# One attention and expert kernel on one core: products of the previous batch, kv and transposes put at other units, and stacking transfers in two pieces

## What is computed

```python
xn = layernorm(x)                                   # x: 8 x 512 x 256
q, k, v = split(xn @ W_qkv.T)                       # 16 heads of 16
q_p = elu(einsum('bhnd,hdf->bhnf', q, proj)) + 1    # 128 features per head
k_p = elu(einsum('bhnd,hdf->bhnf', k, proj)) + 1
kv = einsum('bhnf,bhnd->bhfd', k_p, v)
attn = einsum('bhnf,bhfd->bhnd', q_p, kv)
attn = attn / (einsum('bhnf,bhf->bhn', q_p, k_p.sum(2)) + 1e-8)
a = attn @ W_out.T + b_out
# each token goes to the two best of 8 experts (softmax over the two), 256 -> 1024 -> 256, exact gelu
x + a + ffn(xn)
```

## Time and profile before

| | |
|---|---|
| median of three runs | 743.44 us (743.26 to 744.01) |
| the profiled execution, its own time | 743.44 us |
| its span, first to last instruction | 741.3 us |
| mean granted TensorE clock | 0.993 |
| PE, PEld, DVE, ACT, POOL busy | 95%, 83%, 66%, 64%, 30% of the span |
| transfers | 91.64 MB, mean 124 GB/s |

### The profile page before, as it was taken

How to read it: one execution, slowest core, us unless ns; L and a number is a source line. 1 busy time by engine, 2 the same in 40 slices (tenths; PEclk the granted TensorE clock), 3 DMA queues, 4 the chain that set the end, 5 groups by cost and what they waited for, 6 DMA issues and landing times.

```text
span 741.3 us, 17723 instructions
## 1 busy us (share of the span) xinstructions
PE 704.8 (95%) x5617; PEld 618.0 (83%) x5618; DVE 492.8 (66%) x1281; ACT 476.1 (64%) x879; POOL 223.9 (30%) x165
## 2 busy tenths in 40 slices
PE   8799999999999998799999999999999999999995
PEld 4667777767676866389999999999899999999995
DVE  8898989898989878655556664445666444466443
ACT  5587878787878786675476744456674444666451
POOL 2314141505050504602342222233223323322222
PEclk9999999999999999899999999999999999999998
DMA  8856473737474647526355352334535223443321
GB/s 258 213 140 169 105 222 100 225 98 227 95 229 93 205 96 238 216 89 186 74 82 173 54 157 48 58 76 61 179 55 160 52 44 73 74 132 68 54 44 22
DMA packets 44037, 91.64 MB, mean 124 GB/s; under 512 B 6897, under 2 KB 30193, under 8 KB 41729
## 3 DMA queue, kind: packets, MB, share of 16 engines
q1 hardware_dynamic: 28258, 59.36, 28.3%
q0 software_dynamic: 13872, 18.75, 14.5%
q10 hardware_dynamic: 1872, 13.11, 4.9%
HBM read 39.32 MB, written 26.67 MB: 89 GB/s over the span
## 4 chain that ended last, share of the span: by engine, by line
PE 62%; DVE 19%; issue 10%; ACT 6%; ACTq 1%; DVEq 1%; POOLq 0%
PE F L481 9%; PE F L483 9%; PE F L482 9%; DVE qp L1398 4%; DVE kp L1398 3%; PE NUM L481 3%; PE NUM L482 3%; PE NUM L483 3%; ACT h L1151 3%; PE DEN L481 3%; PE DEN L482 3%; PE DEN L483 3%; PE DEN L555 2%; PE F L543 2%; PE F L537 2%
## 5 line engine op out<-in xcount | busy, mean ns | idle before, releaser
L1151 ACT ACTIVATE h<-F,b1c 128x384 f32<-128x384 f32 x200 | 110.8, 574 | 163.8 <-PE F L483 148.3
L1820 POOL DMA_INDIRECT out<-ysb,icur x75 | 120.4, 1605 | 302.9 <-DVE ysb L1664 288.1
L1641 DVE TENSOR_TENSOR hl<-h,hh 128x768 fp32r<-128x768 f32 x100 | 95.9, 959 | 156.4 <-ACT hh L1155 156.4
L996 ACT ACTIVATE e_ring<-F 128x512 f32<-128x512 f32 x256 | 146.3, 624 | 41.4 <-PE F L537 31.8
L481 PE MATMUL F<-gxh,wh 128*128 128x384 f32 (+1 forms) x400 | 129.8, 325 | 3.9 <-ACT h L1151 1.7
L483 PE MATMUL F<-gxh,wl 128*128 128x384 f32 (+1 forms) x400 | 128.3, 321 | 0.0
L482 PE MATMUL F<-gxl,wh 128*128 128x384 f32 (+1 forms) x400 | 128.3, 321 | 0.0
L1761 POOL DMA_INDIRECT xg<-rows,slots x64 | 63.6, 994 | 179.4 <-PE F L537 144.8
L1398 DVE SCALAR_TENSOR_TENSOR kp<-F,e_ring 128x512 f32<-128x512 f32 x128 | 82.7, 681 | 18.3 <-PE DEN L555 10.5
L1398 DVE SCALAR_TENSOR_TENSOR qp<-F,e_ring 128x512 f32<-128x512 f32 x128 | 85.3, 683 | 6.3 <-ACT e_ring L996 5.9
L1155 ACT ACTIVATE hh<-h 128x768 fp32r<-128x768 f32 x100 | 84.7, 847 | 3.3
(11 more groups left out here) (238 smaller groups left out, 1568.2 us busy)
## 6 DMA issues: line engine op xcount, KB each, us to landing
wraw<-experts ACTq DMA_DIRECT2D x12, 1024.0 KB
grow<-xg SPq DMA_DIRECT2D x26, 408.0 KB
Sk<-kdh SPq DMA_DIRECT2D x64, 128.0 KB, 2.5
Sq<-qdh SPq DMA_DIRECT2D x64, 128.0 KB
xin<-x SPq DMA_DIRECT2D x8, 512.0 KB
Sk<-kdl SPq DMA_DIRECT2D x32, 128.0 KB, 2.4
Sq<-qdl SPq DMA_DIRECT2D x32, 128.0 KB
xres<-x SPq DMA_DIRECT2D x8, 512.0 KB
```

The source lines that it names most:

```text
L996: A(e_ring[:, u % 4, :], F[u % 4][:, :], ACT.Exp, bias=EXP_BIAS, scale=1.0 / DOWN).then_inc(exp_done, 1)
L1151: A(h32[:, m, :], F[m % 4][:, 0:T], ACT.Gelu, bias=b1c[:, w, m:m + 1]).then_inc(gelu, 1)
L1641: V.tensor_tensor(hl[:, 2 * q:2 * q + 2, :], h32[:, 2 * q:2 * q + 2, :], f32(hh[:, 2 * q:2 * q + 2, :]), ALU.subtract).then_inc(hl_rdy, 1)
L1820: pool.indirect_dma_start(out, bass.IndirectOffsetOnAxis(icur[:, s, :], 0), ysb[:, s, :], None, bounds_check=last_token, compute_op=ALU.ad ...
```

## The change

Three things are changed in the attention stage.

1. `stack`: the pairs of heads lie in `Sk` and `Sq` in their plain order. `place_of`, which put the two pairs of one transfer side by side, is gone, in the projections too. A transfer now writes pairs `r` and `r + 4`, so two pieces of 2 KB in each row in place of one of 4 KB. The count and the bytes of the transfers stay; they go out by `r` first, and by part within it.
2. TensorE: `v_logits(b + 1, 0)` and `kv(b, 0)` both follow unit 7 (before unit 8 and unit 9), and `to_tokens(b - 1, 3)` follows unit 13, behind `qk_group(b + 1, 1)` (before unit 15).
3. VectorE, in passes that have a previous batch: reciprocals 0 and 1 with product 0 at unit 3 (before 6), product 1 at 4 (before 7), reciprocal 2 at 8 (before 9), reciprocal and product 3 at 14 (before 17).

```diff
-    def place_of(pair):
-
-        return 2 * (pair % 4) + pair // 4
...
-        for turn in range(len(parts)):
-            for r in range(4):
-                part = parts[(r + turn) % len(parts)]
-                eng.dma_start(dst[32 * part:32 * part + 32, place_of(r):place_of(r) + 2, :].bitcast(F32),
+        for r in range(4):
+            for part in parts:
+                eng.dma_start(dst[32 * part:32 * part + 32, r:PAIRS:4, :].bitcast(F32),
                               src[32 * r:32 * r + 32, :, :].bitcast(F32)).then_inc(done, 16)
...
-                if u == 8:
+                if u == 7:
                     if not first:
                         pe.wait_ge(at_rdy, 4 * b - 3)
                     v_logits(b + 1, 0)
-                if u == 9:
                     if first:
                         pe.wait_ge(pos_read, 1)
                     else:
...
                     qk_group(b + 1, 1)
-                if u == 15:
                     pe.wait_ge(qkl_rdy, 4 * b + 5)
                     if not first:
                         to_tokens(b - 1, 3)
...
-                    if u == 6:
+                    if u == 3:
                         reciprocals(b - 1, 0)
                         reciprocals(b - 1, 1)
                         products(b - 1, 0)
-                    if u == 7:
+                    if u == 4:
                         products(b - 1, 1)
-                    if u == 9:
+                    if u == 8:
                         reciprocals(b - 1, 2)
                     if u == 10:
                         products(b - 1, 2)
-                    if u == 17:
+                    if u == 14:
                         reciprocals(b - 1, 3)
                         products(b - 1, 3)
```

More of the change, by code:

```diff
@@ L536, in unit @@
                     pr = 2 * c + s
-                    last = nc.tensor.matmul(F[c][:, s * D:(s + 1) * D], Sk[0:SROWS, place_of(pr), n * P:(n + 1) * P],
+                    last = nc.tensor.matmul(F[c][:, s * D:(s + 1) * D], Sk[0:SROWS, pr, n * P:(n + 1) * P],
                                             stacked_proj[0:SROWS, 2 * pr:2 * pr + 2, :], start=True, stop=True)
@@ L542, in unit @@
                 h = u - 16
-                last = nc.tensor.matmul(F[h % 4][:, :], stacked_proj[0:SROWS, h, :], Sq[0:SROWS, place_of(h // 2), :],
+                last = nc.tensor.matmul(F[h % 4][:, :], stacked_proj[0:SROWS, h, :], Sq[0:SROWS, h // 2, :],
                                         start=True, stop=True)
```

## The result

The changed kernel takes 746.26 us (median of five, 743.44 to 747.83) against 743.44 (740.77 to 744.01): a ratio of 1.0057, 95% interval 1.0032 to 1.0082. (The ratio isn't that of these two medians: it takes all runs, 17 of the changed kernel with a median of 747.44.) So it is slower by about 0.6%. The forecast was 736.5. The profiled execution took 747.9 us, span 745.7: 4.4 us more than before. Of these, 3.3 us have come together by the first `attend` row of the final pass (starts at 298.55 before, 301.85 after). A pass is measured here from the first `attend` row of one to that of the next.

A forecast was written before the change was run, and what follows sets the result against it. TensorE, 95% busy, bounds the kernel, so only its waits can be won: 5 x (0.74 + 0.51) + 0.74, together 7.0 us off 743.44, with 0.1 given back: 736.5 us, range 735.2 to 740.0.

The forecast's parts named there:

- the two waits: TensorE in attention passes, V group and `at` transposes both waiting for VectorE's products: 0.74 and 0.51 us a pass.
- Second wait: TensorE's transposes of `at`, behind unit 20, wait for product 3 in passes 1 to 5: 0.51 us each.
- First wait: TensorE's V group, behind unit 8 before the change, waits for `at` in passes 1 to 6: 0.74 us each.
- the wait at unit 17: TensorE's unit 17 waits for feature 13, which hangs on exponential 12 behind `kdl`; expected to remain.
- What the group needs is there: VectorE's reciprocals 0 and 1 find their `att` transposes ready; product 0 at 172.5, unit 7 with 0.2 us margin.
- The K remainder and `kdl`: K group 0's remainder starts 0.74 us earlier; the chain through `kdl`, exponential 12 and feature 13 moves with it.
- Second half: VectorE's reciprocal and product 3 before feature 14 remove the whole 0.51 us, at margins of 0.15 and 0.06.
- Rival 1: Transposes of `at` still wait, only the V group's wait goes: gain 4.4 us, 739.0 us; chance 0.21 including what lies between.
- Rival 2: Exponential 8 comes 1.1 us later, features 8 to 11 miss unit 17's slack, gain eaten: 743 us; chance 0.06.
- Rival 3: Stacking transfers in two pieces cost double, 1.24 us each, so Sk and Sq land later: 745.6 us; chance 0.09.
- The clock: TensorE's half-clock stretch at the final pass's end moves by 7 us, may shift the end 1 us either way.

The follow-up runs named there:

- e4: Kernel before with only chunk 3's `att` transposes moved behind K group 1, and reciprocal and product 3 moved before feature 14; 740.65 us, ratio 0.9961.
- e6: Changed kernel with GpSimd's eight indirect sends of passes 1 to 6 moved from the K half into the Q half; 747.24 us, ratio 1.0069.
- e5: Kernel before with GpSimd's eight indirect sends of passes 1 to 6 moved from the K half into the Q half; 749.36 us, ratio 1.0088.
- e3: Kernel before with only V group and `kv` 0 behind unit 7, reciprocals 0 to 2 and products 0 and 1 moved earlier; 745.88 us, ratio 1.0042.
- e10: Changed kernel with the sends of passes 1 to 6 behind units 1, 3, 5, 7, 13, 14, 16, 20; 740.54 us, ratio 0.9999.
- e17: Same kernel as e10, run on another chip; 754.08 us, ratio 1.0157.

## Why the prediction was wrong

- **What bounds the kernel and what the two waits cost** (0.74 and 0.51 us a pass): right. Second wait alone, e4: 0.51. First wait, K half of e6 against e5: 0.64. On C both went, and the gain is 8.7 us, with the wait at unit 17 gone besides; how much each gave there can't be told, since before has no profile on C.
- **"What the group needs is there"**: this step failed first. I took a transpose as ready once TensorE had issued it and the next group was through. On the chips with late posts the second one is posted up to 2.1 us behind its issue, so that product 0 starts at 174.94, where it was to be ready at 172.5 + 1.85 = 174.35; feature 3 stands behind it, and unit 7 is 0.8 us late in these passes, 1.4 in pass 1, whose denser sends I had not looked at. Before, the group started at 173.63, behind all posts, and the lateness showed in no wait row. A margin that I read off engine rows was not one.
- **The K remainder and `kdl`**: this step failed too. I moved `kdl` with the remainder at an unchanged 1.26 us. That figure already held 0.7 us of late post, and by the move it became 2.14, as two sends then covered `kv` 1 instead of one. The chunk 3 transposes, which I had looked at only for what they bring (product 3), wait for this `kdl`: 2.1 us in six passes. I didn't check what the moved instruction itself waits for.
- **Second half**: right by itself, margins of 0.06 and 0.15 us included (e4).
- **Rival 1** (only the first wait goes): the reverse held, only the second could be had. **Rival 2** (the wait moves and nothing is won) is the one that came nearest, and its place was half right: unit 16 waits for feature 13 in e3. Its mechanism wasn't exponential 8 but the posts. I gave it 0.06 and a floor at 743, though nothing in it stops at zero. **Rival 3** (transfers at 1.24 us each): refuted, SP issues eight in 5.11 us against 4.98 before; the slower side came from somewhere I had no rival for.
- **The clock**: half-clock stretches did shift, one more of some 3.4 us in the profiled execution, with TensorE busy for nearly all of it: up to 1.7 us, where I allowed 1. It explains no difference of medians, since the chips' readings above differ in the length of the passes.
- **The forecast on chip C**: the gain there is 8.7 us where I summed 7.0, so the way was right there and the size 1.7 short (the range ended at 8.2). The prediction was made from a profile in which posts are late, and that profile had the evidence: `kv` 0 starts at 175.57 with a row of 1.08 us, and VectorE, idle and released by it, starts feature 8 at 177.26, 1.69 us behind that start.

**Still open:** why the posts are held on A, B and D and hardly on C, and by what path a send on GpSimd delays TensorE's posts. The chip goes with it in all five sets; whether it is the chip or what it held at that time can't be told from these runs. Nor is it told apart whether the send's own instruction does it or the transfer that it starts, since every run moves both. A profile of before on C is missing.

## What to carry to other kernels

Before moving a consumer closer to its producer, measure from the producer's start to the consumer's first possible start in that very stretch, by semaphore events or by the rows of whoever waits; an engine's own row doesn't show when its completion is seen. Follow what each moved instruction waits for, not only who waits for it. And when margins are tenths of a microsecond, compare on more than one chip: the same pair of kernels gave 1.0078 on one and 0.9883 on another.

## What was unexpected in the hardware

- While GpSimd ran an indirect send (0.98 us), TensorE's completion posts were held on three of four chips, mostly until 0.4 to 0.9 us behind the send's end: `kv` posts 2.2 and 3.1 us after its start instead of 1.1, several in one burst. On the fourth the same places show 1.1 us; a few `kv` groups were 0.1 to 0.3 us late, one 0.7.
- An operation of 128 x 4 elements on VectorE took 1.48 us instead of 0.16 beside a GpSimd addition of 128 x 1024 (e10), and 2.88 beside the addition and the copy behind it (e17); it ended within 0.05 us of GpSimd's end.
- The same program differs by 18 us between chips B and C, the kernel before by only 2.8.
